# A state-space block whose scan gets a table for its sums, with ScalarE's mask rows out of four steps and a head in another order

## The chip, the cores and the metric

One NeuronCore of a Trainium2 chip runs the whole program. The metric is device microseconds of one execution, the median of three runs. TensorE (PE), VectorE (DVE), ScalarE (ACT), GpSimd (POOL) and SyncE (SP, which issues all DMAs here) each run their own list of instructions in order and meet at semaphores.

## The reference

Input x is 4 x 32 x 32 x 384 in float32. A group norm is followed by a state-space layer over the 1024 pixels of a picture, in four directions (rows, columns, and both backwards), 192 channels and 16 states:

```python
xz = x @ in_proj_w.T; xh, z = split(xz)
xc = silu(conv3x3_depthwise(xh) + conv_b)
x_dbl = einsum('bkdl,kcd->bkcl', xs, x_proj_w)        # xs: xc in four directions
dts, Bs, Cs = split(x_dbl, [24, 40])
dts = softplus(einsum('bkrl,kdr->bkdl', dts, dt_projs_w) + dt_projs_b)
# per direction, over l:
h = h * exp(d_t * As) + (d_t * u_t) * B_t
y_t = sum_n(h * C_t) + Ds * x_t
# y of the four directions added, layer norm, * silu(z), @ out_proj_w.T
```

The result is added to x, and a second group norm, a router over four experts (top two) and their two-layer networks follow.

## The kernel before

The program has three parts. The **head** normalises x, projects it, convolves it, and writes to HBM, for two pairs of pictures one after the other, the convolved u (in plain and turned order), silu(z), and the projection x_dbl (scratch_xd). The **scan** works through 16 **units**, four for each picture: direction pairs o (rows or columns) and flow s (forwards or backwards), unit u = 4b + 2o + s. The **tail** does the layer norm, the output projection and the experts.

A unit has 24 **steps**. A step is one recurrence over 1024 pixels for 128 pairs of state and channel: step i works on states 2n and 2n+1 (n = i // 3) and on one third of the channels (g = i % 3). What a step needs from each engine:

- ScalarE: the decay, `s_a = exp(dt * A)` (line 1109), issued two steps ahead into a ring of four.
- TensorE: the **spread** of B * dt * u into one of two PSUM buffers `s_pb` (line 1018), 64 small matmuls against the masked matrix `k_area` (called dd in the code). It waits until the scan two steps before has ended.
- VectorE: the **scan** `s_h` (line 1183), which reads both.
- GpSimd: the multiplication of h by C (line 1219), for each group of three steps in two instructions, the first two steps (128x2048) and the third (128x1024).
- TensorE again: the **sum** of the multiplied h into PSUM `s_py` and `s_py2` (add_y, line 1058), each waiting for GpSimd and for the sum before. h has room for four groups, so a scan of group n waits for the sums of group n - 4.

A sum is written behind the spread of a later step: `summed` says how many sums have been issued by step i of unit u. Before, that is seven steps back (LAG), and in the middle of even units up to nine (BEHIND).

In between, each unit makes what the next one needs, as **chunks** that go from TensorE to ScalarE through one PSUM bank `m_pm`: four Z chunks in steps 0 to 3 (line 224: the projection for dt; ScalarE copies it and takes its absolute value, lines 270 and 271), BT in step 4, UT in steps 5, 7, 10 and 13 of odd units (u turned), DUP in steps 16 to 19 (dt for the decays). The softplus of dt is done in three rounds in steps 7, 10 and 13 (ROUND_AT): a logarithm on ScalarE into `m_pm` (line 1095), then four VectorE operations (lines 1157 to 1166), two after each of two scans. After step 15 VectorE forms dt * u (times_u, line 308). The masked matrix dd of a unit has four pieces; GpSimd builds two of them (build_d, line 204: after its group 1, piece 3, and after group 4, piece 1 of the next unit), ScalarE the other two, 64 rows a unit (build_rows, line 298), spread over the steps.

Where a picture's column directions begin or end (take_y), VectorE or ScalarE moves y out of PSUM in step 6, and TensorE adds it back into the new sum in six pieces (carry, at the steps of CARRIES).

In the head the second pair's projections and convolutions are interleaved with unit 0's chunks, and the masked matrix of unit 0 is built by GpSimd as soon as the BT chunk is there. SP's stores follow in a fixed order, and the head ends when every engine is through and every store has landed.

## Time and profile before

| | us |
|---|---|
| median of 3 runs (lowest, highest) | 1583.36 (1574.06, 1601.38) |
| profiled execution | 1595.89 |
| its span, first to last instruction | 1594.1 |
| PE busy | 1351.7 (85%) |
| DVE busy | 1229.5 (77%) |
| POOL busy | 1025.6 (64%) |
| ACT busy | 1018.5 (64%) |

The shares are means over the whole span; the scan, from 188.6 to 1308.3 us, is seven tenths of it, and there VectorE is busy 1006.9 us and GpSimd 1007.0. PE's busy time counts pipelined matmuls and says little by itself. What a row says of a wait names the last instruction that ended it.

### The profile page before, as it was taken

To read this page: it belongs to the slowest core of one execution; us is meant where nothing else is said; L and a number is where in the kernel's file an instruction comes from. 1 tells how busy PE (TensorE), PEld (TensorE's weight loads), DVE (VectorE), ACT (ScalarE), POOL (GpSimd) and SP (SyncE) were. 2 spreads that over 40 slices of the span, in tenths; PEclk is the share of its full clock that TensorE was granted. 3 is DMA by queue.
4 is the path that set the end of the run, shared out by engine and by line. 5 is a ranking of instruction groups with operands and counts; after the bars stand their busy time and mean duration, and the time that the engine had idled before them with its cause. 6 is when DMAs were issued, how large, how long until landed. Compare 5 with 4: busy or idle time off the path is not lost. (4 is left out here: it accounts for less than half of the span.)

```text
span 1594.1 us, 66411 instructions
## 1 busy us (share of the span) xinstructions
PE 1351.7 (85%) x30388; PEld 830.5 (52%) x30388; DVE 1229.5 (77%) x1029; ACT 1018.5 (64%) x1957; POOL 1025.6 (64%) x294
## 2 busy tenths in 40 slices
PE   6997688888987888998788899878889886969998
PEld 5734455554554555555555555545555543535554
DVE  4876198989899898989989997997989884644220
ACT  3448677777778778787877877776787551311222
POOL 0002089989899998999899998988899980000000
PEclk8998879999999999999999999998999997789999
DMA  9243524233333423333342332334243326100111
...
DMA packets 73479, 151.13 MB, mean 95 GB/s; under 512 B 33238, under 2 KB 41942, under 8 KB 72816
## 3 DMA queue, kind: packets, MB, share of 16 engines
...
## 5 line engine op out<-in xcount | busy, mean ns | idle before, releaser
L1219 POOL TENSOR_TENSOR s_h<-s_h,s_crow 128x2048 f32<-128x2048 f32 (+1 forms) x256 | 880.1, 3468 | 159.3 <-DVE s_h L1183 159.3
L1183 DVE TENSOR_TENSOR_SCAN s_h<-s_a,s_pb 128x1024 f32<-128x1024 f32 x384 | 862.4, 2275 | 131.7 <-PE s_pb L1018 96.3
L1018 PE MATMUL s_pb<-k_area,m_dtut 64*64 64x64 f32 x24576 | 479.2, 226 | 149.6 <-DVE s_h L1183 98.7
L1018 PEld LDWEIGHTS s_pb<-k_area,m_dtut 64*64 64x64 f32 x24576 | 435.4, 139 | 325.1 <-DVE s_h L1183 161.9
L1058 PE MATMUL s_py<-s_h,k_eye 64*64 64x512 f32 x3072 | 431.7, 614 | 14.6 <-issue 8.3
L298 ACT ACTIVATE k_area<-k_mask,m_bt 128x64 f32<-128x64 f32 x992 | 273.3, 337 | 0.0
L1109 ACT ACTIVATE s_a<-y_y,m_aneg 128x1024 f32<-128x1024 f32 x192 | 219.0, 1142 | 54.1 <-DVE s_h L1183 53.9
L1109 ACT ACTIVATE s_a<-m_dup,m_aneg 128x1024 f32<-128x1024 f32 x192 | 219.3, 1143 | 32.5 <-DVE s_h L1183 32.5
L204 POOL TENSOR_TENSOR k_area<-m_bt,k_mask 128x2048 f32<-128x2048 f32 x33 | 145.0, 4396 | 128.9 <-ACT m_bt L273 128.9
L1058 PEld LDWEIGHTS s_py<-s_h,k_eye 64*64 64x64 f32 x3072 | 93.2, 138 | 41.4 <-issue 35.6
L270 ACT COPY y_y<-m_pm 128x384 f32<-128x384 f32 x60 | 28.8, 479 | 79.0 <-PE m_pm L224 79.0
L224 PEld LDWEIGHTS m_pm<-k_wdt,k_rows 25*128 25x128 f32 x256 | 43.2, 199 | 59.7 <-issue 59.3
L224 PE MATMUL m_pm<-k_wdt,k_rows 25*128 25x192 f32 x256 | 63.7, 372 | 7.2 <-DMA k_rows<-scratch_xd 7.2
L1504 PE MATMUL t_small<-t_w,k_area 128*128 128x384 f32 x192 | 69.1, 497 | 0.0
L1478 PE MATMUL t_big<-t_xn,t_w 128*128 128x512 f32 x144 | 68.2, 625 | 0.0
L1568 ACT COPY t_out<-t_small 128x384 f32<-128x384 f32 x32 | 15.3, 479 | 82.4 <-PE t_small L1507 82.4
L819 DVE SCALAR_TENSOR_TENSOR h_acc<-h_xpad,h_conv_p,h_acc 128x1024 f32<-128x1024 f32 x48 | 61.7, 1285 | 1.6
L245 PEld LDWEIGHTS m_pm<-k_eye,y_y 64*64 64x64 f32 (+1 forms) x512 | 33.5, 123 | 52.7 <-issue 47.2
L1692 DVE TENSOR_TENSOR k_area<-k_area,t_big 128x1024 f32<-128x1024 f32 x12 | 14.3, 1220 | 47.9 <-PE t_big L1492 47.7
L1504 PEld LDWEIGHTS t_small<-t_w,k_area 128*128 128x128 f32 x192 | 36.5, 194 | 18.2 <-issue 1.2
L245 PE MATMUL m_pm<-k_eye,y_y 64*64 64x64 f32 (+1 forms) x512 | 43.0, 224 | 2.9 <-ACT y_y L273 2.7
L1478 PEld LDWEIGHTS t_big<-t_xn,t_w 128*128 128x128 f32 x144 | 27.8, 200 | 32.4 <-issue 31.9
...
## 6 DMA issues: line engine op xcount, KB each, us to landing
s_crow<-scratch_xd SPq DMA_DIRECT2D x256, 256.0 KB, 4.1
...
```

What stands on the lines that cost most here:

```text
L204: tt(self.dd[:, rows_n].rearrange("p n k j -> p (n k) j"), self.bt[:, u % 2, rows_n].rearrange("p n k -> p (n k)").unsqueeze(2).broadcast_ ...
L224: mm = pe.matmul(pm[:, x * DI:(x + 1) * DI], tokens(rows[0:R + 1], 2 * i + x), self.keep["wdt"][:, o + 2 * s], start=True, stop=True)
L245: mm = pe.transpose(pm[0:chans.stop - chans.start, blk::BLK], self.dt_of[here, blk, chans], eye[here, here])
L298: row = self.nc.scalar.activation(self.dd[:, n, blk], self.keep["mask"][:], ACT.Identity, scale=self.bt[:, u % 2, n, blk:blk + 1])
L819: eng.scalar_tensor_tensor(out, view, w, out, ALU.mult, ALU.add).then_inc(convolved[kind], 1)
L1018: mm = pe.matmul(pb[par * HALF:(par + 1) * HALF, step % 2, r * BANK + blk:(r + 1) * BANK:BLK], dtut[here, u % 2, blk, g * HALF:(g + 1) * H ...
L1058: mm = pe.matmul(dst, eye[here, here], src, start=opens, stop=closes)
L1109: nc.scalar.activation(a[:, step % RING], dup[u % 2][:, g], ACT.Exp, scale=aneg[:, col:col + 1]).then_inc(a_ready, 1)
L1183: nc.vector.tensor_tensor_scan(h[:, step % (TRIPLES * CG), f], a[:, step % RING, f], pb[:, step % 2, f], 0.0, ALU.mult, ALU.add).then_inc( ...
L1219: nc.gpsimd.tensor_tensor(here, here, c.unsqueeze(1).broadcast_to([P, groups.stop - groups.start, L]), ALU.mult).then_inc(hc_ready, 1)
L1478: mm = pe.matmul(big_of("F1", b, j)[:, q], w1[:, c, j * P:(j + 1) * P], xn[:, b % 2, c, q], start=(c == 0), stop=(c == NC - 1))
L1504: pe.matmul(ps, hid[:, j, tok], w2[:, j], start=False, stop=False, skip_group_check=True)
```

## The change

Four things are changed.

1. The sums follow tables, one for unit 0 (SUMS_FIRST), one for even (SUMS_NEW) and one for odd units (SUMS_ON): how many are issued in each step. Steps 0 to 3 have none, some later steps two, and at a unit's end five sums are owed (OWED) in place of seven. The carries move to other steps. In steps 7, 10 and 13 the chunk is issued ahead of the sums.
2. ScalarE's rows of dd follow tables too: none in steps 0 to 5 and 18 and 19, most in 7 to 17 and 20 to 23.
3. The y copies move from step 6 to step 7 (VectorE, now behind the softplus) and 8 (ScalarE); GpSimd's build of piece 1 moves from behind group 4 to behind group 3.
4. In the head the chunks of unit 0 and their exponent, logarithm and softplus come before the second pair's last convolution and projections; two projections of the first pair are done together; one activation table with exponent and logarithm is loaded once; GpSimd waits for dt * u before it builds; SP's stores of the second pair are in another order.

```diff
-BEHIND = {LAG: 1, LAG + 1: 2, LAG + 2: 2, LAG + 3: 1, LAG + 4: 1, LAG + 5: 1}
-CARRIES = {(2, 11): 0, (2, 12): 1, (2, 14): 2, (2, 15): 3, (3, 8): 4, (3, 11): 5}
+OWED = 5
+SUMS_NEW = {4: 1, 5: 1, 6: 2, 7: 1, 10: 1, 11: 2, 12: 1, 13: 2, 14: 2, 15: 2, 16: 1, 17: 1, 18: 1, 19: 1, 20: 1, 21: 1, 22: 2, 23: 1}
+SUMS_ON = {4: 1, 5: 1, 6: 1, 7: 1, 8: 2, 9: 1, 10: 1, 11: 2, 12: 1, 13: 1, 14: 2, 15: 2, 16: 1, 17: 1, 18: 1, 19: 1, 20: 1, 21: 1, 22: 1, 23: 1}
+SUMS_FIRST = {i: 1 for i in range(LAG - 1, STEPS)} | {15: 2}
+CARRIES = {(2, 13): 0, (2, 14): 1, (3, 9): 2, (3, 11): 3, (3, 14): 4, (3, 15): 5}
+TAKE_Y = 7
+ROWS_NEXT = {11: (0, 6), 12: (6, 9), 13: (9, 13), 14: (13, 20), 15: (20, 27), 16: (27, 30), 17: (30, 32)}
+ROWS_SOON = {20: (0, 4), 21: (4, 8), 22: (8, 12), 23: (12, 16)}
+ROWS_LATE = {6: (16, 18), 7: (18, 21), 8: (21, 27), 9: (27, 29), 10: (29, 32)}
...
             x_proj(0, (0,))
             in_proj_x(1, (2,))
+            x_proj(0, (1, 2))
             m.chunk(pe, 0, "Z", 0)
+            in_proj_z(1, range(0, 1))
+            m.chunk(pe, 0, "Z", 1)
             in_proj_x(1, (0,))
-            m.chunk(pe, 0, "Z", 1)
+            m.chunk(pe, 0, "Z", 2)
+            in_proj_z(1, range(1, 2))
+            m.chunk(pe, 0, "Z", 3)
+            x_proj(0, (3,))
             in_proj_x(1, (1,))
-            m.chunk(pe, 0, "Z", 2)
-            x_proj(0, (1,))
-            m.chunk(pe, 0, "Z", 3)
-            x_proj(0, (2,))
             m.chunk(pe, 0, "BT", 0)
...
-            for kind in KINDS:
-                convolve(dve, 1, kind)
+            convolve(dve, 1, 2)
+            convolve(dve, 1, 0)
             lnz, zs, ez, wz = m.lnz, m.zs, m.ez, m.wz
...
             nc.vector.scalar_tensor_tensor(zs, zs, 0.0, lnz, ALU.max, ALU.add).then_inc(m.dt_ready, ROUNDS)
+            convolve(dve, 1, 1)
             m.times_u(dve, 0)
...
             pool.wait_ge(turned, NC * BATCH)
+            pool.wait_ge(m.dtu_ready, 1)
...
             def summed(u, i):
-                held = u > 0 and u % 2 == 0
-                return max(0, u * STEPS + i + 1 - LAG - (BEHIND.get(i, 0) if held else 0))
+                plan = SUMS_FIRST if u == 0 else SUMS_ON if u % 2 else SUMS_NEW
+                return max(0, u * STEPS - OWED) + sum(count for at, count in plan.items() if at <= i)
...
                     spread_b(u, i)
+                    if u + 1 < UNITS and i in ROUND_AT:
+                        chunks_at(u, i)
                     made = summed(u, i)
...
-                    if i == 6 and s == 0 and o == 0 and u:
+                    if i == TAKE_Y + 1 and s == 0 and o == 0 and u:
                         take_y(b - 1)
...
-                    if n == 4 and u + 1 < UNITS:
+                    if n == 3 and u + 1 < UNITS:
                         m.build_d(pool, nc.gpsimd.tensor_tensor, u + 1, 1)
```

Three places show it in the order of instructions. The first is TensorE at the start of unit 1, before; m_pm takes the Z chunk, s_py and s_py2 a sum's two parts, and s_pb the spread.

```order
L1018 MATMUL s_pb<-k_area,m_dtut 64x64 x32
L1058 MATMUL s_py<-s_h,k_eye 64x512 x4
L224 MATMUL m_pm<-k_wdt,k_rows 128x192 x2
L1018 MATMUL s_pb<-k_area,m_dtut 64x64 x32
L1058 MATMUL s_py<-s_h,k_eye 64x512 x2
L1058 MATMUL s_py2<-s_h,k_eye 64x512 x2
L224 MATMUL m_pm<-k_wdt,k_rows 128x192 x2
```

And the same after, in steps 2 to 4 (the spread is line 1020 now, a Z chunk 231, a sum 1060, the BT chunk 235).

```order
L1020 MATMUL s_pb<-k_area,m_dtut 64x64 x32
L231 MATMUL m_pm<-k_wdt,k_rows 128x192 x2
L1020 MATMUL s_pb<-k_area,m_dtut 64x64 x32
L231 MATMUL m_pm<-k_wdt,k_rows 128x192 x2
L1020 MATMUL s_pb<-k_area,m_dtut 64x64 x32
L1060 MATMUL s_py<-s_h,k_eye 64x512 x2
L1060 MATMUL s_py2<-s_h,k_eye 64x512 x2
L235 MATMUL m_pm<-k_eye,k_rows 128x16 x8
```

The sum between spread and Z chunk is gone; the first one stands in step 4. The second place is TensorE in step 7 of unit 1, before.

```order
L1018 MATMUL s_pb<-k_area,m_dtut 64x64 x32
L1058 MATMUL s_py<-s_h,k_eye 64x512 x4
L237 MATMUL m_pm<-k_eye,k_u2 64x64 x2
L239 MATMUL m_pm<-k_eye,k_u01 128x128
L237 MATMUL m_pm<-k_eye,k_u2 64x64 x2
L239 MATMUL m_pm<-k_eye,k_u01 128x128
```

After, with the UT chunk in lines 244 and 246:

```order
L1020 MATMUL s_pb<-k_area,m_dtut 64x64 x32
L244 MATMUL m_pm<-k_eye,k_u2 64x64 x2
L246 MATMUL m_pm<-k_eye,k_u01 128x128
L244 MATMUL m_pm<-k_eye,k_u2 64x64 x2
L246 MATMUL m_pm<-k_eye,k_u01 128x128
L1060 MATMUL s_py<-s_h,k_eye 64x512 x2
L1060 MATMUL s_py2<-s_h,k_eye 64x512 x2
```

The chunk now goes ahead of the sum, so that ScalarE gets it, and with it the bank for its logarithm, one sum earlier. The third place is VectorE at the head's end, before: convolutions of the second pair (lines 816 and 819), the softplus of unit 0 (887 to 893) and its dt * u.

```order
L816 TENSOR_SCALAR h_acc<-h_xpad,h_conv_p 128x1024
L819 SCALAR_TENSOR_TENSOR h_acc<-h_xpad,h_conv_p,h_acc 128x1024 x8
L887 SCALAR_TENSOR_TENSOR y_y<-y_y 128x1536
L889 TENSOR_TENSOR y_y<-y_y 128x1536
L891 SCALAR_TENSOR_TENSOR y_y<-y_y 128x1536
L893 SCALAR_TENSOR_TENSOR y_y<-y_y 128x1536
L308 TENSOR_TENSOR m_dtut<-y_y,m_ut 128x1536
```

After:

```order
L887 SCALAR_TENSOR_TENSOR y_y<-y_y 128x1536
L889 TENSOR_TENSOR y_y<-y_y 128x1536
L891 SCALAR_TENSOR_TENSOR y_y<-y_y 128x1536
L893 SCALAR_TENSOR_TENSOR y_y<-y_y 128x1536
L816 TENSOR_SCALAR h_acc<-h_xpad,h_conv_p 128x1024
L819 SCALAR_TENSOR_TENSOR h_acc<-h_xpad,h_conv_p,h_acc 128x1024 x8
L315 TENSOR_TENSOR m_dtut<-y_y,m_ut 128x1536
```

The softplus goes ahead of the third convolution.

## Rows read from the trace of the kernel before

**Rows 1.** Windows: us, busy time of PE, PEld, DVE, ACT, POOL; clock, DMA.

```profile
263.60:1244.50 980.90, 840.39 (x25316) 522.95 (x25312) 885.20 (x527) 756.00 (x1552) 891.89 (x254) 0.97 0.35 89
```

**Rows 2.** Waits: engine, line, releaser; us in total, times, longest.

```profile
POOL s_h L1219 <- DVE s_h L1183: 159.3, 62, 56.4
...
DVE s_h L1183 <- PE s_pb L1018: 96.3, 123, 5.0
...
PE s_pb L1018 <- issue: 43.3, 47, 2.4
...
DVE m_pm L1157 <- ACT m_pm L1095: 12.6, 10, 2.3
```

**Rows 3.** Time line of VectorE in unit 8: start, us, instruction, idle before.

```profile
756.51 2.29 DVE L1183 TENSOR_TENSOR_SCAN s_h<-s_a,s_pb 128x1024 f32<-128x1024 f32 x1 [0.51 <-PE s_pb L1018]
...
762.10 2.29 DVE L1183 TENSOR_TENSOR_SCAN s_h<-s_a,s_pb 128x1024 f32<-128x1024 f32 x1 [0.51 <-PE s_pb L1018]
...
764.65 6.64 DVE L1183 TENSOR_TENSOR_SCAN s_h<-s_a,s_pb 128x1024 f32<-128x1024 f32 x3 [0.26 <-PE s_pb L1018]
773.57 0.69 DVE L1157 SCALAR_TENSOR_TENSOR m_pm<-s_wz,m_pm 128x512 f32<-128x512 f32 x1 [2.28 <-ACT m_pm L1095]
```

**Rows 4.** Time line of TensorE in steps 2 and 3 of unit 8.

```profile
755.28 1.16 PE L1018 MATMUL s_pb<-k_area,m_dtut 64*64 64x64 f32 x64
756.27 1.04 PE L1058 MATMUL s_py<-s_h,k_eye 64*64 64x512 f32 x8
757.24 0.91 PE L224 MATMUL m_pm<-k_wdt,k_rows 25*128 25x192 f32 x4
758.08 1.16 PE L1018 MATMUL s_pb<-k_area,m_dtut 64*64 64x64 f32 x64
```

**Rows 5.** Time line of GpSimd in unit 8.

```profile
771.37 3.63 POOL L204 TENSOR_TENSOR k_area<-m_bt,k_mask 128x2048 f32<-128x2048 f32 x1
...
792.21 6.85 POOL L1219 TENSOR_TENSOR s_h<-s_h,s_crow 128x2048 f32<-128x2048 f32 x2 [2.32 <-DVE s_h L1183]
799.03 5.19 POOL L204 TENSOR_TENSOR k_area<-m_bt,k_mask 128x2048 f32<-128x2048 f32 x1
...
818.07 4.54 POOL L1219 TENSOR_TENSOR s_h<-s_h,s_crow 128x2048 f32<-128x2048 f32 x1 [0.20 <-DVE s_h L1183]
```

**Rows 6.** Time line of VectorE at the head's end.

```profile
129.76 1.75 DVE L887 SCALAR_TENSOR_TENSOR y_y<-y_y 128x1536 f32<-128x1536 f32 x1
...
138.57 4.99 DVE L893 SCALAR_TENSOR_TENSOR y_y<-y_y 128x1536 f32<-128x1536 f32 x1
```

**Rows 7.** Time line of ScalarE at the head's end.

```profile
153.89 1.14 ACT L726 ACTIVATE h_xc<-h_acc,h_conv_p 128x1024 f32<-128x1024 f32 x1
...
173.68 1.00 ACT L740 COPY h_dbl<-h_big 32x1024 f32<-32x1024 f32 x1
...
181.85 3.91 ACT L298 ACTIVATE k_area<-k_mask,m_bt 128x64 f32<-128x64 f32 x16
```

**Rows 8.** Time line of TensorE in unit 10, steps 10 and 11: two sums, a carry.

```profile
916.28 1.09 PE L1058 MATMUL s_py<-s_h,k_eye 64*64 64x512 f32 x8
917.55 1.09 PE L1058 MATMUL s_py<-s_h,k_eye 64*64 64x512 f32 x8 [0.18 <-PE s_py L1058]
918.46 1.16 PE L1018 MATMUL s_pb<-k_area,m_dtut 64*64 64x64 f32 x64
...
920.57 1.11 PE L1028 MATMUL s_py<-y_y,k_eye 128*128 128x256 f32 x2
```

**Rows 9.** Time line of TensorE at the lower clock, units 0 and 8.

```profile
199.25 1.64 PE L224 MATMUL m_pm<-k_wdt,k_rows 25*128 25x192 f32 x4
...
777.24 1.98 PE L1018 MATMUL s_pb<-k_area,m_dtut 64*64 64x64 f32 x64 [3.86 <-DVE s_h L1183]
```

**Rows 10.** Windows: start of unit 13; steps 16 to 23 of unit 8.

```profile
1096.50:1112.00 15.50, 13.56 (x230) 8.17 (x231) 6.94 (x5) 6.22 (x15) 11.66 (x4) 0.67 0.28 71
800.70:821.00 20.30, 16.62 (x536) 10.29 (x528) 17.70 (x10) 15.25 (x32) 20.10 (x6) 1.00 0.69 162
```

More of the change, by code:

```diff
@@ L483, in head @@
         order = [("T", b, c) for b in range(3) for c in range(NC)] + [("X", 0, kind) for kind in KINDS]
-        order += [("T", 3, c) for c in range(NC)] + [("P", 0, 0)] + [("X", 1, kind) for kind in KINDS]
-        order += [("P", 0, at) for at in range(1, PROJ)] + [("P", 1, at) for at in range(PROJ)]
+        order += [("T", 3, c) for c in range(NC)] + [("P", 0, 0), ("X", 1, 2), ("P", 0, 1), ("P", 0, 2), ("X", 1, 0), ("P", 0, 3), ("X", 1, 1)]
+        order += [("P", 1, at) for at in range(PROJ)]
         def big_of(*use):
@@ L545, in _ @@
             store_u(1, 0)
-            store_u(1, 1)
             store_z(1, 0, TT // 2)
-            store_xd(1, 0)
-            store_xd(1, 1)
-            store_xd(1, 2)
-            store_xd(1, 3)
             m.double(sp, 0, range(CG))
             store_z(1, TT // 2, TT)
+            store_u(1, 1)
+            for at in range(PROJ):
+                store_xd(1, at)
             for b in range(BATCH):
@@ L763, in _ @@
             fill_xpad(1, 2)
+            take_xd(0, 1)
             for b in range(2, BATCH):
@@ L767, in _ @@
             m.take_chunk(act, 0, "Z", 0)
+            take_xd(0, 2)
+            silu_z(1, range(0, 1))
+            m.take_chunk(act, 0, "Z", 1)
             fill_xpad(1, 0)
-            m.take_chunk(act, 0, "Z", 1)
-            fill_xpad(1, 1)
             m.take_chunk(act, 0, "Z", 2)
-            take_xd(0, 1)
+            silu_z(1, range(1, 2))
             m.take_chunk(act, 0, "Z", 3)
-            for part in range(3):
-                m.exponent(act, 0, part)
-            act.wait_ge(m.exp_ready, 1)
+            act.preload_act_table_set("natural_log_exp_and_others")
+            m.exponent(act, 0, 0)
+            m.exponent(act, 0, 1)
+            take_xd(0, 3)
+            m.exponent(act, 0, 2)
             nc.scalar.activation(m.lnz, m.ez, ACT.Ln, bias=1.0).then_inc(m.ln_ready, ROUNDS)
@@ L1061, in summed, with chunks_at @@
             def summed(u, i):
-                held = u > 0 and u % 2 == 0
-                return max(0, u * STEPS + i + 1 - LAG - (BEHIND.get(i, 0) if held else 0))
+                plan = SUMS_FIRST if u == 0 else SUMS_ON if u % 2 else SUMS_NEW
+                return max(0, u * STEPS - OWED) + sum(count for at, count in plan.items() if at <= i)
+            def chunks_at(u, i):
+                for what in chunks_of(u + 1):
+                    if chunk_slot(*what) == i:
+                        m.chunk(pe, u + 1, *what)
             for u in range(UNITS):
@@ L1074, in _ @@
                         carry(u // 4, CARRIES[u % 4, i], made)
-                    if u + 1 < UNITS:
-                        for what in chunks_of(u + 1):
-                            if chunk_slot(*what) == i:
-                                m.chunk(pe, u + 1, *what)
-                    elif 6 <= i < 6 + TT:
+                    if u + 1 < UNITS and i not in ROUND_AT:
+                        chunks_at(u, i)
+                    elif u == LAST_U and 6 <= i < 6 + TT:
                         t = i - 6
@@ L1085, in _ @@
                         norm.turn(pe, pm, t)
-            for step in range(LAST - LAG, LAST):
+            for step in range(summed(LAST_U, STEPS - 1), LAST):
                 add_y(step // CG, step % CG)
@@ L1198, in _ @@
                             m.times_u(dve, u + 1)
+                    if i == TAKE_Y and s == 0 and o == 1:
+                        take_y(b)
                     if u == LAST_U and i == 0:
```

57 lines of the change are left out of this document (21 added, 36 removed).

## The prediction, made before the changed kernel had run

> **What bounds the kernel now.** I read the views in this order: the busy time by stage, the waits, then the order in time of one unit, engine by engine. By stage, the fourteen units 1 to 14 of the scan take 980.9 us, 70.1 us each, with VectorE busy 885.2 and GpSimd 891.9 [rows 1]: 63.2 and 63.7 us a unit. So two engines are some 90% busy, neither is full, and 6.4 us a unit is the most that a better order inside the scan can take out before GpSimd is the wall. The waits say who stops whom [rows 2]: VectorE's scan waits for TensorE's spread (s_pb) 96.3 us in all; GpSimd's multiplication waits for the scans 159.3 us, of which 56.4 is the head; TensorE itself stood 43.3 us in front of spreads with no releaser shown; and the softplus waited for its logarithm 12.6 us in ten places.
>
> In time, in the z-chunk steps of unit 8 a scan starts every 2.79 us, with 0.51 us of waiting before each, where three in a row elsewhere take 6.64 us, 2.2 each [rows 3]. TensorE fills those 2.79 us to the end: spread 755.28 to 756.27, sum of y to 757.24, z chunk 0.84 to the next spread, 0.99 + 0.97 + 0.84 = 2.80 [rows 4]. So these four steps belong to TensorE, and the rest of the unit to VectorE and GpSimd. GpSimd needs 6.85 us for a group of three steps, against 6.6 for three bare scans [rows 3, 5].
>
> **The change part by part.** The sum is made against the profiled execution, 1595.9 us, which lies 12.5 us over the median of the three runs, 1583.4; I take the same saving off both.
>
> *Sums out of steps 0 to 3.* TensorE then has 0.99 + 0.84 = 1.83 us in a step, under VectorE's 2.2, and the step falls from 2.79 to 2.2. ScalarE has decay, copy and absolute value there and loses its mask rows, so it is not next. 0.59 x 4 steps x 14 units = **33 us**. Unit 0 had no sums there, and gains nothing. Ends: 17 (half, if TensorE then waits for GpSimd in the sums) and 33.
>
> *Steps 4 to 6.* Step 4 takes 2.55 us where 2.2 would do, with the BT chunk on TensorE [rows 3]. TensorE now enters it early by up to a microsecond, since a spread may be that late before a scan waits: 0.35 x 14 = 4.9, and more where a UT chunk follows in step 5. Even units pay back with two sums in step 6. I take **6 us**, between 0 and 10.
>
> *UT chunk before the sum in steps 7, 10, 13, and the y copies a step later.* In unit 8 the softplus waited 2.28 us for its logarithm [rows 3]: ScalarE's copy of the last batch's y stood in front of it, waiting for sums. In odd units the UT chunk stood behind a sum of 0.97. Both are moved out of the way; the whole **12.6 us** [rows 2] should go, since the next thing late there is the scan itself. Ends 6 and 12.6.
>
> *Stalls at the unit's start.* Where the clock is at its lower level in these steps, spread, sum and chunk all double: in unit 13 the first 15.5 us ran at 0.67 of full clock [rows 10]. With the sum gone a third of that work is. The waits for s_pb outside the regular 0.51 x 4 x 14 = 28.6 come to 68 us, unit 0's among them; most lie in steps 16 to 23, which gain nothing. I take **4 us**, between 0 and 15.
>
> *What is paid for it.* The sums come back elsewhere: two in a step cost 1.27 + 0.97, the second waiting for the first (916.28 to 917.55, [rows 8]). In softplus steps VectorE has some 3.5 us of its own (2.2 and two operations of 0.69, [rows 3]), which covers that. In step 22 of even units it isn't: 0.99 + 2.24 = 3.2 against 2.2, less the microsecond of lead, 0.6 x 7 = 4. From step 15 on the sums run five or six steps behind the spread, where it was seven. GpSimd has steps 3n and 3n+1 multiplied 4.54 us after the second scan at best [rows 5]; sum 3n at a lag of five is asked for two scans and a spread later, 4.4 + 1.0. That leaves 0.9 us, and GpSimd falls behind by 0.25 a group: 4 us over the units, between 0 and 17. Unit 15 has no chunks that would gain, but its sums of steps 0 to 3 and two carries are now in steps 8 to 15, beside the norm's transposes: four sums of 1.27 and carries of 1.11 [rows 8], about 5, and 1 for carries elsewhere. Together **14 us**, between 5 and 22.
>
> *GpSimd's mask build a group earlier.* It takes 5.19 us beside VectorE's product dt * u after step 15 and 3.63 us alone, and there is a gap of 2.32 us before group 4, into which it now moves [rows 5]. By the rows alone 1.56 us a unit would be won, 22 us of GpSimd's time over fourteen units and at most that off the sum. I count 0: the product then falls on a multiplication of h, and whatever reads beside it loses the same. The Trainium skill says so too (SBUF — State Buffer, Who interferes with whom): a VectorE operation with two SBUF inputs and a GpSimd operation that reads SBUF exclude each other for the whole instruction; by it nothing is won either.
>
> *ScalarE's rows by table.* The same 64 rows a unit, in softplus steps, where ScalarE has room. Piece 2's last rows come in step 10 and TensorE needs them in step 12; two scans of lead cover that. Nothing; without that cover some 1 us a unit.
>
> *The head.* In it unit 0's chain ran behind all three convolutions of the second pair (softplus from 129.76), and two of its operations took 4.99 us beside GpSimd's builds instead of 1.75 [rows 6]. Now one convolution comes behind the softplus and the builds wait for the product. Worked through instruction by instruction with the durations of before, an estimate: the second convolution ends at about 122 (its input now stands behind two of the first pair's projections), the logarithm at 123.3, four operations of 1.76 give dt at 130.6 instead of 143.6, the last convolution (11.3) ends at 141.9. ScalarE, not VectorE, then sets the pace: silus, UT and DUP copies fill it until 153.3, where the silu of the last convolution starts, at 153.89 before [rows 7]. From there the projections and their copies run to 174.68, 20.8 us. Before, DUP copies and z tiles of 7.2 us followed, then 3.91 of rows; now only the rows. End 153.3 + 20.8 + 3.9 = 178.0 against 185.8: **8 us**. Ends 0 (ScalarE's round trips to TensorE longer, 8 us of them guessed at high clock) and 14.
>
> Sum: 33 + 6 + 12.6 + 4 + 8 - 14 = 49.6. The profiled execution would take 1546 us, the median **1534 us**, 3.1% less. The tail is untouched.
>
> **The rivals.**
> *GpSimd takes the wall over.* The sums now ask so early that TensorE waits in front of a sum, with the next spread behind it in its queue and the scan behind that. For it: 0.9 us of room, one slow build is 1.56. Against: units were 6.4 us above GpSimd's busy time, and in the new order they still would be some 3. Priced at the far ends above: 17 + 3 + 9 + 2 + 6 - 20 = 17, or 1566 us; with half of that 1555.
>
> *The head gives nothing.* Then 1542, still faster.
>
> *Everything that waits is TensorE's.* If the leads absorb the other stalls too, steps run at GpSimd's pace: 33 + 10 + 12.6 + 15 + 14 - 5 = 80, or 1504 us.
>
> *The clock falls in the emptied steps.* TensorE now idles 0.4 us in each of four steps. At the lower level (1.2 GHz) a spread takes 1.98 (here it fell after an idle of 3.86 us) and a chunk 1.64 us [rows 9], so 3.5 us a step instead of 2.79 before: 0.7 x 4 lost, and in the three steps behind it spread and sum 3.9 instead of about 2.4, 4.5 more. Such a unit loses 7.3 us instead of winning its 2.8 of the two first terms. It decides from five units on (49.6 / 10.1); with all fourteen, 1534 + 141 = 1675, with eight, 1615. Against it: steps 16 to 23, with 1.95 of TensorE in 2.2, ran at 1.00 [rows 10]. The Trainium skill has the rule that speaks for it (TensorE: Matmul & The Clock Gate, A second HAM failure mode: psum-queue depth-cycling): many short idles between groups of matmuls made the clock swing between its levels. No run here shows that for idles this short.
>
> *It doesn't do what it says*, since TensorE isn't what the z steps wait for: ruled out by [rows 4] as far as rows can, and held with the first rival.
>
> **How the numbers follow.** My forecast has a chance of 0.55 (1517 to 1551), GpSimd's wall 0.20, of which a quarter still under the bound, the head giving nothing 0.07, the best case 0.10, the clock 0.08. Two per cent, 31.7 us (the three runs of before lie 27 apart, so less can't be told), is at 1551.7. Faster: 0.55 less 0.05 for its rim, 0.05, 0.07, 0.10, together 0.72. Slower by over 2%: 0.07. Within: 0.21. The range goes from the best case to the first rival with all its far ends: 1504 to 1568.
>
> **What would show each step.** In the profile of the changed kernel: scans in steps 0 to 3 every 2.2 us with no wait before them; VectorE's wait for s_pb near 60; no wait of the softplus for its logarithm in ten places; the first scan near 180; units of some 66.5 us. GpSimd as a releaser of sums (s_py waiting for s_h) over 30 us would mean the first rival; a granted clock under 0.93 in units 1 to 14 the clock. It is wrong if the scans of steps 0 to 3 stay at 2.8 us, or if TensorE's idles without a releaser grow.

## The result, and the profile after

The changed kernel takes 1618.0 us (median of 4 runs, 1606.22 to 1633.47) against 1586.6 for the kernel before (4 runs, 1574.06 to 1601.38). The ratio is 1.0182, 95% interval 1.0130 to 1.0235: it is slower, and whether by more than 2% can't be told. I had forecast 1534 us, and a range up to 1568. Medians here and below are of all executions, but ratios leave out those more than 1.5% above the fastest of their kernel, among them the profiled executions of the changed kernel (1633.5 us) and of two experiments below, e7 and e9.

Units 1 to 14 of the scan take 1017.0 us where they took 980.9 [rows 1], and their granted clock is 0.91 where it was 0.97. The windows of the changed kernel (columns as in [rows 1]): these units, four steps of unit 2, three of unit 3, and a piece of the head.

```profile
264.38:1281.40 1017.02, 898.88 (x25329) 577.16 (x25333) 902.74 (x527) 752.46 (x1547) 868.54 (x253) 0.91 0.34 86
...
332.37:341.40 9.03, 8.22 (x280) 6.49 (x278) 8.81 (x5) 7.35 (x12) 9.03 (x3) 1.00 0.28 88
405.97:416.50 10.53, 10.53 (x207) 9.08 (x208) 7.78 (x4) 5.73 (x9) 7.96 (x4) 0.55 0.18 53
...
162.00:176.00 14.00, 8.56 (x18) 2.66 (x16) 0.00 (x0) 5.06 (x6) 0.00 (x0) 0.76 0.36 146
```

Its waits, against [rows 2]: the scan waits for spreads 129.3 us instead of 96.3, GpSimd for scans 209.1 instead of 159.3.

```profile
POOL s_h L1222 <- DVE s_h L1186: 209.1, 73, 41.7
...
DVE s_h L1186 <- PE s_pb L1020: 129.3, 137, 5.3
...
PE s_pb L1020 <- issue: 47.8, 42, 2.9
```

**The emptied steps.** VectorE's time line shows both faces of the change: in unit 2 four scans in a row (steps 2 to 5), 2.2 us each, as forecast; in unit 3, from its second step on, a scan every 3.5 us with 1.2 us of waiting, where [rows 3] had 2.79 and 0.51. The last three rows are of unit 8: the scan of step 15, the product dt * u behind it, and the next scans.

```profile
337.02 8.96 DVE L1186 TENSOR_TENSOR_SCAN s_h<-s_a,s_pb 128x1024 f32<-128x1024 f32 x4 [0.21 <-PE s_pb L1020]
...
405.97 2.29 DVE L1186 TENSOR_TENSOR_SCAN s_h<-s_a,s_pb 128x1024 f32<-128x1024 f32 x1 [1.47 <-PE s_pb L1020]
408.58 2.29 DVE L1186 TENSOR_TENSOR_SCAN s_h<-s_a,s_pb 128x1024 f32<-128x1024 f32 x1 [0.33 <-PE s_pb L1020]
412.09 2.29 DVE L1186 TENSOR_TENSOR_SCAN s_h<-s_a,s_pb 128x1024 f32<-128x1024 f32 x1 [1.22 <-PE s_pb L1020]
...
821.55 2.29 DVE L1186 TENSOR_TENSOR_SCAN s_h<-s_a,s_pb 128x1024 f32<-128x1024 f32 x1
823.75 2.90 DVE L315 TENSOR_TENSOR m_dtut<-y_y,m_ut 128x1536 f32<-128x1536 f32 x1
826.57 4.45 DVE L1186 TENSOR_TENSOR_SCAN s_h<-s_a,s_pb 128x1024 f32<-128x1024 f32 x2
```

TensorE's time line in the same stretch of unit 3 shows what TensorE did there (it answers to [rows 4]). It idles 1.69 us at the unit's start, the clock falls to its lower level at 406.9, and from there spread (1.99) and z chunk (1.64) follow each other without a gap: 3.5 us a step, TensorE busy 10.53 us of 10.53. The first sum of y comes at 418.77, still at the lower level, and the spread behind it runs at full clock again.

```profile
405.12 0.80 PE L1020 MATMUL s_pb<-k_area,m_dtut 64*64 64x64 f32 x37 [1.69 <-issue]
405.85 0.91 PE L231 MATMUL m_pm<-k_wdt,k_rows 25*128 25x192 f32 x4
406.70 1.84 PE L1020 MATMUL s_pb<-k_area,m_dtut 64*64 64x64 f32 x64
408.47 1.64 PE L231 MATMUL m_pm<-k_wdt,k_rows 25*128 25x192 f32 x4
410.04 1.99 PE L1020 MATMUL s_pb<-k_area,m_dtut 64*64 64x64 f32 x64
...
417.01 1.99 PE L1020 MATMUL s_pb<-k_area,m_dtut 64*64 64x64 f32 x64
418.77 1.93 PE L1060 MATMUL s_py<-s_h,k_eye 64*64 64x512 f32 x8
420.63 0.67 PE L235 MATMUL m_pm<-k_eye,k_rows 16*128 16x16 f32 x8
421.23 1.16 PE L1020 MATMUL s_pb<-k_area,m_dtut 64*64 64x64 f32 x64
```

In this execution nine such falls begin between step 23 of a unit and step 1 of the next, and last 10.2 to 20.5 us; the others, in later steps, last 3.4 or 6.8. Added up over units 1 to 15 the lower clock holds for 184 us, against 58 before.

**Step 15.** The 16 products dt * u take 2.88 us in the mean, 1.73 before, and the softplus waits for its logarithm no longer (12.6 in [rows 2]); groups of VectorE's instructions:

```profile
L315 DVE TENSOR_TENSOR m_dtut<-y_y,m_ut 128x1536 f32<-128x1536 f32 x16 | 46.0, 2876 | 2.8 <-ACT m_ut L280 2.8
...
L1160 DVE SCALAR_TENSOR_TENSOR m_pm<-s_wz,m_pm 128x512 f32<-128x512 f32 x45 | 30.5, 678 | 0.0
```

GpSimd's time line, the same steps of unit 8. The build takes 3.64 us in the gap ahead of group 4 (it was 5.19 behind it, [rows 5]), so group 4 begins 818.15 and is still being multiplied when the product comes at 823.75; GpSimd then waits 3.96 us in front of group 5, and has won nothing.

```profile
814.57 3.64 POOL L211 TENSOR_TENSOR k_area<-m_bt,k_mask 128x2048 f32<-128x2048 f32 x1
818.15 6.89 POOL L1222 TENSOR_TENSOR s_h<-s_h,s_crow 128x2048 f32<-128x2048 f32 x2
828.99 6.87 POOL L1222 TENSOR_TENSOR s_h<-s_h,s_crow 128x2048 f32<-128x2048 f32 x2 [3.96 <-DVE s_h L1186]
```

**The head.** The first scan starts at 185.78, 2.8 us earlier. ScalarE, against [rows 7]: the last silus start at 155.88 (worked out: 153.3), and the last projections' copies end only at 179.05, since the second half of them waited 8.61 us.

```profile
155.88 1.15 ACT L728 ACTIVATE h_xc<-h_acc,h_conv_p 128x1024 f32<-128x1024 f32 x1
...
174.95 1.01 ACT L741 COPY h_dbl<-h_big 96x1024 f32<-96x1024 f32 x1 [8.61 <-PE h_big L648]
...
179.05 3.92 ACT L305 ACTIVATE k_area<-k_mask,m_bt 128x64 f32<-128x64 f32 x16
```

TensorE stood 4.36 us in front of these projections, and its clock fell (0.76 in the last window above); one took 3.75 us that takes 1.98 at full clock.

```profile
166.60 3.75 PE L644 MATMUL h_big<-h_xc,h_wx 128*128 128x512 f32 x4 [4.36 <-ACT h_dbl L746]
...
171.88 1.98 PE L644 MATMUL h_big<-h_xc,h_wx 128*128 128x512 f32 x4
```

**Where the time is.** For each kernel I took the interval from one scan's start to the next, less the pace that VectorE's own work sets (2.2 us; 3.5 in softplus steps; 3.85 in step 15; a y copy of 1.95), and added it up over units 1 to 14. From before to changed the five columns of steps add up to 36 us: -4, +19, -12, +17 and +16. Low clock is its time in units 1 to 15; the table has the kernels of the experiments too. All in us, from one profiled execution each.

| kernel | first scan | units 1-14 | steps 0-3 | 4-6 | 7-14 | 15 | 16-23 | low clock |
|---|---|---|---|---|---|---|---|---|
| before | 188.6 | 980.8 | 46.4 | 11.1 | 13.7 | -0.1 | 30.4 | 58 |
| changed | 185.8 | 1017.0 | 42.2 | 30.2 | 2.1 | 16.5 | 46.6 | 184 |
| e1 table, build late | 186.4 | 990.7 | 24.8 | 25.2 | 4.4 | 16.2 | 40.8 | 120 |
| e2 wide filler | 188.1 | 1016.8 | 53.5 | 16.0 | 2.8 | 18.3 | 46.9 | 75 |
| e3 narrow filler | 186.4 | 1028.4 | 60.1 | 27.2 | 3.0 | 15.9 | 43.0 | 188 |
| e4 old sums | 188.9 | 992.3 | 44.4 | 11.1 | 2.6 | 18.8 | 36.0 | 79 |
| e5 old sums, build late | 190.2 | 958.1 | 35.2 | 11.3 | 2.8 | 0.2 | 29.3 | 31 |
| e6 before + early build | 189.7 | 997.9 | 40.5 | 10.7 | 14.5 | 16.2 | 36.7 | 75 |
| e7 two sums kept | 187.7 | 997.3 | 50.2 | 15.9 | 3.6 | 9.1 | 39.2 | 140 |
| e8 before + chunk first | 193.0 | 968.3 | 40.7 | 11.0 | 14.4 | -0.1 | 22.9 | 62 |
| e9 table, build behind product | 185.9 | 1004.6 | 36.1 | 33.8 | 3.3 | 2.2 | 50.0 | 167 |
| e10 e7, build behind product | 190.2 | 969.8 | 37.5 | 14.1 | 2.7 | 2.2 | 34.0 | 93 |
| e11 before + rows | 188.0 | 963.4 | 37.3 | 11.3 | 6.8 | -0.1 | 28.7 | 34 |
| e12 before + head | 186.2 | 974.9 | 40.4 | 11.2 | 13.8 | 0.2 | 29.9 | 48 |

### The profile page after: what moved, and what is told of

Read it like the earlier page. It is cut to its first block and busy times, and to the rows that moved or that the text cites. A ratio compares the mean times of both kernels' runs of the same rounds, so it can differ in the third digit from the quotient of the medians.

```text
span 1631.7 us, 66413 instructions
## 1 busy us (share of the span) xinstructions
PE 1405.3 (86%) x30388; PEld 879.1 (54%) x30388; DVE 1242.1 (76%) x1029; ACT 1014.3 (62%) x1955; POOL 1000.6 (61%) x294
## 5 line engine op out<-in xcount | busy, mean ns | idle before, releaser
L1222 POOL TENSOR_TENSOR s_h<-s_h,s_crow 128x2048 f32<-128x2048 f32 (+1 forms) x256 | 880.8, 3468 | 209.3 <-DVE s_h L1186 209.1
L1186 DVE TENSOR_TENSOR_SCAN s_h<-s_a,s_pb 128x1024 f32<-128x1024 f32 x384 | 862.6, 2275 | 171.8 <-PE s_pb L1020 129.3
L1020 PEld LDWEIGHTS s_pb<-k_area,m_dtut 64*64 64x64 f32 x24576 | 463.4, 146 | 303.7 <-issue 169.5
L1020 PE MATMUL s_pb<-k_area,m_dtut 64*64 64x64 f32 x24576 | 502.0, 233 | 127.7 <-DVE s_h L1186 69.2
L1060 PE MATMUL s_py<-s_h,k_eye 64*64 64x512 f32 x3072 | 442.2, 632 | 21.9 <-PE s_py L1060 12.5
L305 ACT ACTIVATE k_area<-k_mask,m_bt 128x64 f32<-128x64 f32 x992 | 261.0, 335 | 0.0
L211 POOL TENSOR_TENSOR k_area<-m_bt,k_mask 128x2048 f32<-128x2048 f32 x33 | 119.8, 3632 | 143.2 <-DVE m_dtut L315 143.2
L231 PE MATMUL m_pm<-k_wdt,k_rows 25*128 25x192 f32 x256 | 78.8, 441 | 5.7 <-DMA k_rows<-scratch_xd 4.4
L1507 PE MATMUL t_small<-t_w,k_area 128*128 128x384 f32 x192 | 69.2, 497 | 0.0
L231 PEld LDWEIGHTS m_pm<-k_wdt,k_rows 25*128 25x128 f32 x256 | 54.0, 242 | 14.0 <-issue 8.8
L315 DVE TENSOR_TENSOR m_dtut<-y_y,m_ut 128x1536 f32<-128x1536 f32 x16 | 46.0, 2876 | 2.8 <-ACT m_ut L280 2.8
L1507 PEld LDWEIGHTS t_small<-t_w,k_area 128*128 128x128 f32 x192 | 36.7, 195 | 18.2 <-issue 1.2
```

The costliest lines, as they stand in the source:

```text
L211: tt(self.dd[:, rows_n].rearrange("p n k j -> p (n k) j"), self.bt[:, u % 2, rows_n].rearrange("p n k -> p (n k)").unsqueeze(2).broadcast_ ...
L231: mm = pe.matmul(pm[:, x * DI:(x + 1) * DI], tokens(rows[0:R + 1], 2 * i + x), self.keep["wdt"][:, o + 2 * s], start=True, stop=True)
L305: row = self.nc.scalar.activation(self.dd[:, n, blk], self.keep["mask"][:], ACT.Identity, scale=self.bt[:, u % 2, n, blk:blk + 1])
L1020: mm = pe.matmul(pb[par * HALF:(par + 1) * HALF, step % 2, r * BANK + blk:(r + 1) * BANK:BLK], dtut[here, u % 2, blk, g * HALF:(g + 1) * H ...
L1060: mm = pe.matmul(dst, eye[here, here], src, start=opens, stop=closes)
L1186: nc.vector.tensor_tensor_scan(h[:, step % (TRIPLES * CG), f], a[:, step % RING, f], pb[:, step % 2, f], 0.0, ALU.mult, ALU.add).then_inc( ...
```

## The experiments

The theory after the result: two losses, each on its own. A: without sums in steps 0 to 3 TensorE's clock, once fallen at a unit's start, stays down until sums return. B: the build one group earlier leaves GpSimd in a multiplication when the product comes. The rivals to A are that the idle time in the emptied steps keeps the clock down, or that the steps wait for something else and the clock follows from that; the rival to B that the product is slow for what the table does elsewhere. The ratio is to the kernel before on the same chip.

| run | edit | median us | ratio (95%) |
|---|---|---|---|
| e1 | changed, build behind group 4 again | 1610.3 | 1.0203 (1.0135-1.0271) |
| e2 | changed, 128x512 product more per z chunk | 1636.3 | 1.0345 (1.0283-1.0407) |
| e3 | changed, first z matmul twice | 1659.1 | 1.0465 (1.0377-1.0552) |
| e4 | changed, sums, carries, y copies as before | 1607.2 | 1.0157 (1.0102-1.0213) |
| e5 | e4, build behind group 4 again | 1572.3 | 0.9901 (0.9870-0.9932) |
| e6 | before, build behind group 3 | 1614.7 | 1.0166 (1.0115-1.0217) |
| e7 | e1, a sum in steps 0 and 2 | 1591.5 | 1.0006 (0.9967-1.0045) |
| e8 | before, UT chunk ahead of the sum, a y copy later | 1587.8 | 1.0012 (0.9990-1.0034) |
| e9 | e1, build waits for the product | 1604.1 | 1.0069 (1.0029-1.0110) |
| e10 | e7, build waits for the product | 1585.3 | 0.9978 (0.9943-1.0012) |
| e11 | before, ScalarE's rows by the tables | 1577.2 | 0.9959 (0.9925-0.9993) |
| e12 | before, the head | 1581.0 | 1.0011 (0.9980-1.0042) |

**e1, the build back behind group 4.**

```diff
-                    if n == 3 and u + 1 < UNITS:
+                    if n == 4 and u + 1 < UNITS:
```

> The changed kernel with GpSimd's build of piece 1 back behind group 4. Theory B (the moved build makes VectorE's product dt * u meet a multiplication that GpSimd has already begun, and wait for it): the product goes from 2.88 us back to 1.73, the step after it from about 5.0 to 3.85 us, 15 x 1.15 = 17 us less, and a few falls of the clock in step 17 fewer: 1618 to about 1598. Rival (the build's place is free, all of the loss is the clock in steps 0 to 3): within 5 us of 1618.

A miss: the time lies between the two forecasts, and step 15 kept its 16.2 us. Only its form changed: the product is back at 1.73 us in most units, and five of the fourteen carry the whole loss, with products of 4.6 to 5.1 us. The time lines of VectorE and of GpSimd show how, first in unit 3 of e1, then the product and the build in unit 3 of the kernel before.

```profile
441.82 2.29 DVE L1186 TENSOR_TENSOR_SCAN s_h<-s_a,s_pb 128x1024 f32<-128x1024 f32 x1 [0.29 <-PE s_pb L1020]
444.02 4.67 DVE L315 TENSOR_TENSOR m_dtut<-y_y,m_ut 128x1536 f32<-128x1536 f32 x1
```

```profile
436.61 6.88 POOL L1222 TENSOR_TENSOR s_h<-s_h,s_crow 128x2048 f32<-128x2048 f32 x2 [1.93 <-DVE s_h L1186]
443.46 3.61 POOL L211 TENSOR_TENSOR k_area<-m_bt,k_mask 128x2048 f32<-128x2048 f32 x1
```

```profile
452.92 1.73 DVE L308 TENSOR_TENSOR m_dtut<-y_y,m_ut 128x1536 f32<-128x1536 f32 x1
```

```profile
452.96 5.17 POOL L204 TENSOR_TENSOR k_area<-m_bt,k_mask 128x2048 f32<-128x2048 f32 x1
```

In e1 the build was first by 0.56 us, about half of it the 0.29 us that the scan of step 15 had waited for a spread; the product, 4.67 us long, ended 1.6 us after the build. In the kernel before the product was first, by 0.04 us here and by 0.01 to 0.05 us in every unit, and it was the build that took 5.17 us. So it is a race for who is first, won by a few hundredths of a microsecond. The Trainium skill says this (SBUF — State Buffer, Who interferes with whom): a VectorE operation with two SBUF inputs and a GpSimd operation that reads SBUF exclude each other, and the order of issue decides who waits. The rows agree.

**e2 and e3, more work for TensorE in the emptied steps.** Both compute the same outputs; e2's product goes into the tile that the z chunk then overwrites, e3 does the chunk's first matmul twice.

```diff
+            if u:
+                pe.matmul(pm[:], self.keep["eye"][:], self.keep["gavg"][:, 0:4].rearrange("p a b -> p (a b)"), start=True, stop=True)
```

```diff
-            for x in range(2):
+            for x in (0, 0, 1) if u else (0, 1):
```

> The changed kernel with one matmul of 128x512 (result overwritten by the chunk) ahead of each Z chunk, some 0.43 us of TensorE at full clock, so 2.26 us in steps 0 to 3. Theory A (the loss is the clock, which sits at its lower level in the steps that the sums left): the granted clock in units 1 to 14 goes from about 0.92 back to 0.96 or more, steps 0 to 3 take some 2.3 to 2.5 us in place of mostly 3.5, steps 4 to 6 lose their 1.4 us a unit, 1618 to about 1580. Rival R (the steps are held up by waits of TensorE on GpSimd or on its instructions, and the clock follows from these): more work on TensorE, so 0 to 15 us more than 1618.

> The changed kernel with the first matmul of each Z chunk done twice (the same result), again some 0.42 us of TensorE more in steps 0 to 3. Theory A1 (the idle of 0.4 us a step lets the clock fall): as the wide one, about 1580. Theory A2 (idle isn't what decides; at the lower level these steps run without any idle and stay there): steps at the lower level grow from 3.5 to some 4.3 us, in about eight units of fourteen, 25 us more: about 1640.

Windows over units 1 to 14, and two rows of TensorE's time line each; first e2, then e3:

```profile
269.27:1286.05 1016.78, 905.46 (x25432) 558.59 (x25434) 904.99 (x528) 752.21 (x1547) 872.10 (x254) 0.96 0.34 86
```

```profile
1001.44 1.12 PE L231 MATMUL m_pm<-k_gavg,k_eye 128*128 128x512 f32 x2
1002.49 0.91 PE L233 MATMUL m_pm<-k_wdt,k_rows 25*128 25x192 f32 x4
```

```profile
265.81:1294.24 1028.43, 915.62 (x25438) 599.49 (x25440) 902.23 (x528) 753.21 (x1547) 872.84 (x254) 0.91 0.33 85
```

```profile
407.73 1.99 PE L1020 MATMUL s_pb<-k_area,m_dtut 64*64 64x64 f32 x64
409.65 2.28 PE L231 MATMUL m_pm<-k_wdt,k_rows 25*128 25x192 f32 x6
```

The wide filler brings the clock back (0.96; low 75 us instead of 184) and steps 4 to 6 with it (16.0 us over their pace instead of 30.2); the narrow one does not (0.91; 188). By its time e2 is a miss: 1636, where A had said 1580 and R at most 1633. I had the filler's price wrong, 1.05 us instead of 0.43, so it fills more than the room it stands in, and the time grows; what speaks for A is the clock and steps 4 to 6, not the time. e3's slow steps take 4.1 us, about what A2 had said; its time, 1659, lies 19 us over. That idle time alone keeps the clock down is out: in e3's slow steps TensorE goes from one instruction to the next without any. The two fillers differ in length as well (1.05 us at full clock; 2.28 - 1.64 = 0.64 us at the lower one), so these runs don't say which of their properties matters.

**e4 and e5, the old sums, with the early build and with the late one.**

```diff
-CARRIES = {(2, 13): 0, (2, 14): 1, (3, 9): 2, (3, 11): 3, (3, 14): 4, (3, 15): 5}
-TAKE_Y = 7
+BEHIND = {LAG: 1, LAG + 1: 2, LAG + 2: 2, LAG + 3: 1, LAG + 4: 1, LAG + 5: 1}
+CARRIES = {(2, 11): 0, (2, 12): 1, (2, 14): 2, (2, 15): 3, (3, 8): 4, (3, 11): 5}
+TAKE_Y = 6
...
-                plan = SUMS_FIRST if u == 0 else SUMS_ON if u % 2 else SUMS_NEW
-                return max(0, u * STEPS - OWED) + sum(count for at, count in plan.items() if at <= i)
+                held = u > 0 and u % 2 == 0
+                return max(0, u * STEPS + i + 1 - LAG - (BEHIND.get(i, 0) if held else 0))
...
```

> The changed kernel with the sums, carries and y copies of the kernel before; head, ScalarE's rows, the earlier build and the chunk ahead of the sum in steps 7, 10 and 13 stay. Theory A: steps 0 to 3 back at 2.8 us at full clock; less 7 for the logarithm, less 3 for the head, plus 17 for the build against the kernel before: about 1593. Rival (the table isn't the loss, the build and the head are): 1610 to 1620.

> The changed kernel with the sums, carries and y copies in the steps of before and the mask build behind GpSimd's group 4 again; what is left of the change is the head, ScalarE's rows by the table and the UT chunk in front of the sum in steps 7, 10 and 13. If the sums by the table and the earlier build are the two losses: product dt * u in step 15 back near 1.75 us (3.0 with the old sums and the early build), steps 7 to 14 without the wait for the logarithm (2 to 4 us over their pace in units 1 to 14 instead of 13.7), the first scan at 186 to 189 us, and a time 8 to 14 us below before, 1567 to 1573. If the earlier build is harmless and something of the rows or the chunk order costs the time in step 15: still 1600 to 1608.

e4: the clock is back (low 79 us) and most of steps 0 to 3 take 2.8 us again, but step 15 costs 18.8. Its 1607.2 is 14 us over what theory A gave and 3 short of the rival's range. e5: step 15 at 0.2 and the product at 1.75, as in the group below; the time lies within its first forecast, though the first scan (190.2) does not. It is the version that beats both, 0.990 of the kernel before. Between e5 and e4 stands the early build alone, 2.6% by the ratios, some 40 us where I had taken 17; between e5 and e1 the table with what it does to the race, 3.0%.

```profile
L1161 DVE SCALAR_TENSOR_TENSOR m_pm<-s_wz,m_pm 128x512 f32<-128x512 f32 x45 | 30.5, 678 | 1.7 <-ACT m_pm L1103 1.7
...
L316 DVE TENSOR_TENSOR m_dtut<-y_y,m_ut 128x1536 f32<-128x1536 f32 x16 | 28.0, 1747 | 4.3 <-ACT m_ut L281 4.3
```

**e6, the early build in the kernel before.**

```diff
-                    if n == 4 and u + 1 < UNITS:
+                    if n == 3 and u + 1 < UNITS:
```

> The kernel before with one edit, GpSimd's build of the next unit's first d piece behind group 3 instead of group 4. If the product of step 15 then meets a multiplication of h already in flight: product 2.8 to 3.0 us instead of 1.73, the intervals of step 15 some 15 to 19 us over their pace in units 1 to 14, and a time 15 to 25 us above before, 1596 to 1606, with the granted clock as before. By my prediction, which counted this move at nothing: 1580, and the product unchanged.

B holds by itself: 1.0166, some 26 us (15 to 25 forecast), step 15 at 16.2, and the product's group at 2.86 us.

```profile
L308 DVE TENSOR_TENSOR m_dtut<-y_y,m_ut 128x1536 f32<-128x1536 f32 x16 | 45.7, 2855 | 9.3 <-ACT m_ut L273 9.3
```

This profile also has something against A as it is worded. In unit 0, where no sum has been issued yet, the clock rose at 213.0, behind two spreads in a row (208.53 to 212.22) and 0.9 us ahead of the first sum. So a sum is not the only thing behind which it comes back.

```profile
212.92 1.18 PE L1018 MATMUL s_pb<-k_area,m_dtut 64*64 64x64 f32 x64 [0.70 <-DVE s_h L1183]
213.93 1.03 PE L1058 MATMUL s_py<-s_h,k_eye 64*64 64x512 f32 x8
```

**e7, two of the four sums kept.**

```diff
-OWED = 5
-SUMS_NEW = {4: 1, 5: 1, 6: 2, 7: 1, 10: 1, 11: 2, 12: 1, 13: 2, 14: 2, 15: 2, 16: 1, 17: 1, 18: 1, 19: 1, 20: 1, 21: 1, 22: 2, 23: 1}
...
+OWED = 7
+SUMS_NEW = {0: 1, 2: 1, 4: 1, 5: 1, 6: 2, 7: 1, 10: 1, 11: 2, 12: 1, 13: 2, 14: 2, 15: 2, 16: 1, 17: 1, 18: 1, 19: 1, 20: 1, 21: 1, 22: 1}
...
```

> The changed kernel with the build late, and with two of the sums kept in the z-chunk steps: one in step 0 and one in step 2, two fewer at the end of a unit (seven owed instead of five). If the clock falls because TensorE's work in these steps has no sums in it: with a sum in every second step the clock stays up in most units, lower-clock time in units 1 to 15 60 to 90 us instead of 120 to 185, steps 4 to 6 back near 11 us over their pace instead of 25, and a time of 1580 to 1592. If half of the sums don't hold it: clock below 0.92, lower-clock time over 110 us, and 1605 to 1615 as with the build late alone.

1591.5, the rim of the first expectation: steps 4 to 6 came back to 15.9. But the lower clock held for 140 us in the profiled execution (1608.1, the longest of ten), more than the 110 of the second. Over its ten runs the mean granted clock of the whole program goes from 0.918 to 0.936 and the time from 1608 to 1576 with it; in e1 the clock was 0.907 to 0.921, in the kernel before, beside e7, 0.935 and more. So a sum in every second step holds the clock in part. Some of the gain over e1 is the race: step 15 fell from 16.2 to 9.1.

**e9 and e10, the product always first.** e9 is e1, e10 is e7, each with one line:

```diff
                     if n == 4 and u + 1 < UNITS:
+                        pool.wait_ge(dtu_ready, u + 2)
```

> The changed kernel (table of sums with none in steps 0 to 3), with the mask build behind group 4 and a wait in front of it for the product dt * u, so that the product always goes first. If the loss in step 15 is only who of the two goes first: product 1.75 us in every unit, step 15 within 3 us of its pace over units 1 to 14 instead of 16.2, and a time of 1588 to 1600; what is then left above the kernel with the old sums and the late build (1572) is what the table of sums costs by itself, with the granted clock still at 0.91 to 0.93. If the wait costs GpSimd as much as the product loses: 1605 to 1615.

> The kernel with a sum kept in steps 0 and 2, with the same wait in front of the build. If both causes are as told: step 15 within 3 us of its pace instead of 9, the clock at 0.925 to 0.935 as without the wait, and 1578 to 1586. If the wait costs as much as it saves: 1588 to 1596.

The product is back at 1.75 us in both, step 15 at 2.2. e10's 1585.3 lies in its first range; e9's median lies between its two ranges, while its ratio, which makes 1597, falls in the first. e9 leaves the table by itself against e5: 1.0069 to 0.9901, 27 us, with the late race taken out. Its units split by the clock; two windows, units 4 and 12, which stand at the same place in the program's round of four units:

```profile
468.05:534.02 65.97, 56.75 (x1786) 37.02 (x1785) 62.26 (x39) 53.70 (x110) 60.77 (x19) 0.97 0.39 98
1038.57:1114.02 75.45, 66.13 (x1785) 43.37 (x1785) 63.01 (x38) 54.00 (x110) 60.22 (x18) 0.84 0.38 92
```

The six units with at most 6.8 us of lower clock took 66.0 to 69.8 us, 67.8 in the mean; the eight others 72.3 to 79.5, mean 74.7. Of the 7.0 us between them 6.5 lie in steps 0 to 6. In e5, with 31 us of lower clock in all, the same six units take 67.5 in the mean and the same eight 69.2.

**e8, e11 and e12, what the rest is worth.** The chunk ahead of the sum (and ScalarE's y copy in step 7), the rows by the tables, the head, each alone in the kernel before; the edits are the parts of the change's diff of these names.

```diff
+                    if u + 1 < UNITS and i in ROUND_AT:
+                        for what in chunks_of(u + 1):
+                            if chunk_slot(*what) == i:
+                                m.chunk(pe, u + 1, *what)
                     made = summed(u, i)
...
```

```diff
-                        if 6 <= i < 18:
-                            m.build_rows(act, u + 1, 0, share(i - 6), share(i - 5))
...
+                        if i in ROWS_NEXT:
+                            m.build_rows(act, u + 1, 0, *ROWS_NEXT[i])
...
```

```diff
-            for kind in KINDS:
-                convolve(dve, 1, kind)
+            convolve(dve, 1, 2)
+            convolve(dve, 1, 0)
...
+            convolve(dve, 1, 1)
             m.times_u(dve, 0)
...
```

> The kernel before with two edits: in steps 7, 10 and 13 the UT chunk stands in front of the sum on TensorE, and ScalarE's copy of the last batch's y comes in step 7 instead of 6. If the whole gain of the kernel with the old sums and the late build (0.990) is the logarithm that no longer waits: steps 7 to 14 at 2 to 4 us over their pace instead of 13.7, and a time 10 to 16 us below before, 1571 to 1577. If the head and ScalarE's rows by the table have a part in it: 1577 to 1585.

> The kernel before with one edit, ScalarE's mask rows by the three tables instead of two or three in every step. The chunk in front of the sum took nothing off the softplus' wait for its logarithm (13.0 us after it, 12.6 before). If it is the rows in ScalarE's queue that the logarithm stood behind: that wait under 4 us, and 1570 to 1578. If it takes rows and chunk order together, or the head: the wait over 6 us, and 1578 to 1586. My prediction counted the rows at nothing.

> The kernel before with the head of the changed kernel alone (unit 0's chain in front of the second pair's projections, the mask builds behind the product). By my prediction the first scan comes 8 us earlier, and 1578. From the first scans of the kernels that have this head, 185.8 to 190.2 us against 188.6 before and 193.0 with the old head: 0 to 5 us earlier, 1581 to 1586.

The softplus' wait for the logarithm, first in e8, then in e11:

```profile
L1161 DVE SCALAR_TENSOR_TENSOR m_pm<-s_wz,m_pm 128x512 f32<-128x512 f32 x45 | 30.6, 679 | 13.0 <-ACT m_pm L1099 13.0
```

```profile
L1160 DVE SCALAR_TENSOR_TENSOR m_pm<-s_wz,m_pm 128x512 f32<-128x512 f32 x45 | 30.5, 678 | 5.6 <-ACT m_pm L1098 5.6
```

The chunk alone takes nothing off it or off the time, against both of its expectations. The rows alone take 7.0 us off, fewer than expected, and 0.4% of the time; with the chunk and the head as well (e5) 1.7 are left, of the y copy in front of the logarithm in units 4 and 8. The head alone brings the first scan 2.4 us forward (186.2) and does not show in the time. Which of the three together make the rest of e5's 1.0% was not tried.

## Why the prediction was wrong

**The step that failed first: "Sums out of steps 0 to 3", and the chance of 0.08 beside it.** The kernel was to win 33 us there, 4 more in stalls and 6 in steps 4 to 6. It won 4 in steps 0 to 3 and lost 19 in 4 to 6. What failed in the step is that 1.83 us of TensorE holds at full clock alone; where the clock falls at a unit's start, a step takes 3.5 us. That is the rival that I had written down with its price: 3.5 us a step, three slow steps behind it, 7.3 us a unit where the clock falls, eight units giving 1615. The units of e9 put the loss at 74.7 less 69.2 in the same units of e5, 5.6 us a unit. That 1615 lies beside the measured 1618 is luck: the rival's sum has the head's 8 us, which did not come, and nothing for the mask build, which cost more than that; and the execution in which nine units had a long fall took 1633.5. How many fall differs: three in the profiled execution of e1, seven in that of e9, with the same table. With the old sums it was one in the kernel before (unit 13, [rows 10]) and none in e4.

The chance was wrong because I argued from idle time and looked for idles as short as 0.4 us. The evidence lay in a row that I had used for another purpose: the z chunk at 199.25 in [rows 9] is of unit 0, where there are no sums yet. The window and the time line there, of the kernel before, show the very mix of work that the change gives to units 1 to 14:

```profile
184.90:215.60 30.70, 24.58 (x568) 20.79 (x572) 17.80 (x8) 23.67 (x45) 13.64 (x4) 0.50 0.33 77
```

```profile
192.30:210.87 18.57, 18.57 (x408) 16.12 (x408) 10.79 (x5) 13.57 (x29) 8.91 (x3) 0.50 0.28 68
```

```profile
202.74 1.64 PE L224 MATMUL m_pm<-k_wdt,k_rows 25*128 25x192 f32 x4
204.31 1.99 PE L1018 MATMUL s_pb<-k_area,m_dtut 64*64 64x64 f32 x64
...
213.33 1.93 PE L1058 MATMUL s_py<-s_h,k_eye 64*64 64x512 f32 x8
215.04 1.14 PE L1018 MATMUL s_pb<-k_area,m_dtut 64*64 64x64 f32 x48
```

The clock is at its lower level for 30.7 us. For 18.57 of them, from 192.30, spreads and chunks run end to end without lifting it, and it rises just behind the first sum. The counter-evidence that I weighed, full clock in steps 16 to 23 [rows 10], had a sum in every step. The rule that I quoted (the Trainium skill, TensorE: Matmul & The Clock Gate, A second HAM failure mode: psum-queue depth-cycling) lays the swing to short idles between groups; here an idle of 0.7 to 2.3 us stands ahead of each of the nine long falls, though one of 1.34 us at the start of unit 9 brought none. But the clock then stays down through a stretch with no idle in it at all, and of that the rule says nothing.

**"What is paid for it", 14 us, was too small.** In the six units of e9 with the clock up, steps 0 to 3 do run at 2.2 us, and take 2.1 us less than in the same units of e5; yet these units are no shorter as a whole (67.8 us against 67.5). What was won is given back where I had looked for it, 1.9 us of it in steps 16 to 23, the rest in the other steps, the carries of units 3 and 11 among them. So these profiles show no gain of the table even with the clock up, where I had 29 us (33 + 6 + 4 - 14).

**"GpSimd's mask build a group earlier", counted 0, was a loss of 26 us by itself (e6).** I had seen that the product would fall on a multiplication of h, and held that GpSimd had paid before and somebody would pay the same after. But GpSimd's 1.56 us were paid in front of a group with slack, and VectorE's 1.15 x 14 = 16 us are on the path; the gap filled ahead of group 4 opened again ahead of group 5. Steps 16 to 23 show 6 us more in e6; the rest stands in no column of the table, for the kernel before had been profiled in an execution 12.5 us over its median. That in its old place, too, who pays hangs on a lead of 0.01 to 0.05 us, I did not see at all.

**The 12.6 us of the logarithm were right in size and wrong in cause.** Steps 7 to 14 fell from 13.7 to 2.1 us over their pace. But the edit that I gave it to does nothing alone (e8), and "ScalarE's rows by table", counted 0, does over half of it (e11): ScalarE works through its list in order, and rows that stand ahead of the absolute value and the logarithm make both late. Rows, chunk and head together are e5, 1.0% under the kernel before.

**The head, 8 us, gave 2.8 in the trace and nothing in the time (e12).** The chain came near at first: dt done at 130.9 (worked out 130.6). Two pieces then failed by about the same. The silu of the last convolution started 2.6 us late (155.88 instead of 153.3). And "From there the projections and their copies run to 174.68, 20.8 us" was taken over as a fixed length, but they took 23.2 (to 179.05). Before, DUP chunks and z tiles stood between the projections on TensorE, which idled 1.57 us in front of the second half, and its clock was 1.00 in that stretch; without them it idled 4.36 us and did the next projections in part at the lower clock. This is my "Ends 0" for the reason that I named in brackets.

**Rivals.** GpSimd's wall is not the main loss: GpSimd is busy less (868.5 us in units 1 to 14, 891.9 before) and waits more. But it came nearer than I had held: the weight loads of sums waited for it 26.2 us in all, 5.6 before, just under my 30. Its price was wrong too: the far ends as I had given them make 17 + 0 + 6 + 0 + 0 - 22 = 1, or 1582, not 1566, and halfway to 1566 is 1550, not 1555. The measured time lies outside even so. What stays open is which property of the work decides over the clock. In these runs it came back behind sums and behind the wide filler, and stayed down through spreads with z chunks, whether or not TensorE idled; once, in e6, it came back behind spreads alone. Why the same code held the clock in unit 4 of e9 and not in unit 12 was not tried either.
